# Eight experts on lists of the chosen tokens instead of on all tokens, and a first phase ordered by layer

## The reference

```python
def _ffn(x, wi, bi, wo, bo):
    return jax.nn.selu(x @ wi + bi) @ wo + bo
xf = x.reshape(-1, Hh)                                  # 2048 tokens of 128
gate_logits = _ffn(xf, gate_wi, gate_bi, gate_wo, gate_bo)   # 128 logits a token
topv, topi = jax.lax.top_k(gate_logits, K)              # K = 2 of 128
topv = topv / jnp.sum(topv, axis=-1, keepdims=True)
onehot = (topi[..., None] == jnp.arange(E)).astype(x.dtype)  # E = 8 experts
w = jnp.einsum('nk,nke->ne', topv, onehot)
h = jax.nn.selu(jnp.einsum('nh,ehf->enf', xf, exp_wi) + exp_bi[:, None, :])
out_e = jnp.einsum('enf,efh->enh', h, exp_wo) + exp_bo[:, None, :]
out = jnp.einsum('enh,ne->nh', out_e, w)
```

## Time and profile before

| | |
|---|---|
| median of 3 runs | 2991.18 us (2987.4 to 2996.92) |
| span of the profiled execution | 2973.9 us |
| PE busy | 2455.8 us (83%) |
| DVE busy | 2084.7 us (70%) |
| ACT busy | 1434.7 us (48%) |
| POOL busy | 560.2 us (19%) |
| DMA | 49.96 MB, mean 17 GB/s |

### The profile page before, as it was taken

How to read it: one execution, slowest core, us unless ns; L and a number is a source line. 1 busy time by engine, 2 the same in 40 slices (tenths; PEclk the granted TensorE clock), 3 DMA queues, 4 the chain that set the end, 5 groups by cost and what they waited for, 6 DMA issues and landing times. The chain is left out here.

```text
span 2973.9 us, 42131 instructions
## 1 busy us (share of the span) xinstructions
PE 2455.8 (83%) x16214; PEld 1563.1 (53%) x16214; DVE 2084.7 (70%) x4048; ACT 1434.7 (48%) x2603; POOL 560.2 (19%) x482
## 2 busy tenths in 40 slices
PE   5789897886797677897978869967778989789889
PEld 1257574454586322675744546835555554555554
DVE  6988887998998999998879976575572142652331
ACT  5533335884652365333358866445234434335342
POOL 2710001224792037000012205600010100000100
PEclk8999998998887679999979989978889999899999
DMA  3000000110000000000021110002000000000000
GB/s 156 0 1 1 1 1 24 42 43 12 1 1 1 0 1 0 1 28 8 1 85 42 43 62 11 2 0 52 29 1 1 1 2 1 8 1 1 1 2 7
DMA packets 28888, 49.96 MB, mean 17 GB/s; under 512 B 5264, under 2 KB 18320, under 8 KB 28176
## 3 DMA queue, kind: packets, MB, share of 16 engines
q1 hardware_dynamic: 26384, 45.17, 5.0%
q10 hardware_dynamic: 2304, 2.10, 0.3%
HBM read 26.94 MB, written 1.44 MB: 10 GB/s over the span
## 5 line engine op out<-in xcount | busy, mean ns | idle before, releaser
L146 PEld LDWEIGHTS ps<-held_ffn,hidden 128*128 128x128 f32 x2304 | 301.0, 192 | 142.4 <-issue 122.7
L164 ACT ACTIVATE grown<-ps,bias_grown 128x512 f32<-128x512 f32 x288 | 197.9, 687 | 310.5 <-PE ps L146 310.5
L146 PE MATMUL ps<-held_ffn,hidden 128*128 128x128 f32 x2304 | 305.2, 276 | 9.8 <-DVE hidden L183 9.8
L177 POOL TENSOR_TENSOR qk<-conv,held_const 128x512 f32<-128x512 f32 x64 | 89.7, 1402 | 944.4 <-DVE conv L183 944.4
L183 DVE SCALAR_TENSOR_TENSOR conv<-conv_in,held_l1a,conv 128x512 f32<-128x512 f32 x288 | 235.6, 838 | 18.7 <-ACT conv L164 15.9
L177 POOL TENSOR_TENSOR long<-long,product 128x512 f32<-128x512 f32 x136 | 198.3, 1511 | 124.5 <-ACT product L164 122.8
L183 DVE SCALAR_TENSOR_TENSOR hidden<-ps,bias_kept,grown 128x512 f32<-128x512 f32 x288 | 215.0, 748 | 7.3
L180 DVE TENSOR_SCALAR grown<-grown,bias_fallen 128x512 f32<-128x512 f32 x288 | 138.5, 481 | 59.5 <-ACT grown L164 53.2
L177 POOL TENSOR_TENSOR part<-state,c_rows 128x512 f32<-128x512 f32 x128 | 162.8, 1297 | 81.5 <-issue 34.7
L207 POOL MEMSET wide_q<- 128x1536 f32 x8 | 11.0, 1378 | 833.2 <-DVE stream_b L180 783.4
L146 PE MATMUL ps<-part,held_const 128*128 128x512 f32 x256 | 147.3, 674 | 6.9 <-POOL part L177 4.6
(11 more groups left out here) (456 smaller groups left out, 5477.5 us busy)
## 6 DMA issues: line engine op xcount, KB each, us to landing
turned<-conv SPq DMA_DIRECT2D x256, 64.0 KB, 2.0
ring<-lags SPq DMA_DIRECT2D x64, 128.0 KB
held_ffn<-in_ffn SPq DMA_DIRECT2D x1, 4690.0 KB, 17.9
held_l1a<-in_l1a SPq DMA_DIRECT2D x2, 2120.0 KB, 15.5
held_l3f<-in_l3f SPq DMA_DIRECT2D x1, 2824.0 KB, 12.2
yT<-y ACTq DMA_DIRECT2D x16, 128.0 KB, 4.9
out<-x SPq DMA_DIRECT2D x4, 256.0 KB, 2.6
held_rows<-in_rows SPq DMA_DIRECT2D x1, 788.5 KB, 7.2
```

What stands on the lines that cost most here:

```text
L146: ins = self.real.matmul(out, lhsT, rhs, **kw)
L164: return self.sent(self.real.activation(out, a, func, **kw), 0.13 + columns(out) / 1150, 0.14)
L177: return self.vector(self.real.tensor_tensor(out, a, b, op), columns(out), out, a, b)
```

## The change

1. `experts` takes both pairs of a stream at once (1024 tokens). The gate runs as before: 8 units a call.
2. A routing step follows. VectorE takes the two best logits and their places (`max`, `max_index`), builds one-hot marks, and counts with two small matmuls and two scans how many choices fall on each expert. Every choice gets a slot number; the slots of one expert fill whole tiles of 128, 23 tiles being enough in the worst case. A choice that fell on no expert gets a slot behind the 23 tiles.
3. POOL writes the normalized tokens to their slots in the chip's memory with 16 indirect DMAs of 128 rows of 512 bytes (`scatter`). SP reads the 23 tiles back (`xg`).
4. Each of the 23 tiles is one unit of another shape: 4 matmuls 128x128 up with 4 small bf16 matmuls for the bias, one exponential, one `fall` and one `selu` of 128x512, 4 matmuls 128x128 down with one bf16 matmul. Before it SP reads the tile's expert from SBUF into a register (`value`) and loads that expert's weights, 512 KB, into a ring of three places. All 23 tiles run, whether they hold tokens or not.
5. The results go to the chip's memory, and POOL fetches each choice's row with 16 indirect DMAs (`gather`). VectorE adds them to x with their weights, 16 instructions.
6. The first phase runs layer by layer: both pairs of a stream, then the next layer. The windowed attention's weights are loaded once, the filter's matrices `l2p` after both streams' second pair has left that layer. `project_channels` has two pairs in each stream in place of three and one.

The core of the diff:

```diff
+SLOT_TILES = 23
+W_RING = 3
+CHUNK = 4
+X_GROUP = [0, 0, 1, 1, 1, 1]
+SLICES = [(q, min(CHUNK, SLOT_TILES - q)) for q in range(0, SLOT_TILES, CHUNK)]
...
+        def up(j):
+            W = R.ring[:, j % W_RING, :]
+            yield pe.wait_ge(s.kept_x, j // CHUNK + 1)
+            yield pe.wait_ge(R.w_loaded[j % W_RING], w_at(j))
...
+            for c in range(FC):
+                out = tile(st.ps(j % 2), c)
+                pe.matmul(out, tile(W, c), tile(b.xgT[:, j // CHUNK % 2, :], j % CHUNK), start=True, stop=False)
+                mm = pe.matmul(out, tile(m.bias16[0:SPLIT, :], c), pick(j), start=False, stop=True)
+            mm.then_inc(s.up)
+
+        def down(j):
...
+            yield pe.wait_ge(s.hidden, GATE + j + 1)
+            if j:
+                yield pe.wait_ge(s.y_kept, j)
+            for c in range(FC):
+                pe.matmul(st.ps(2)[:, 0:P], tile(hidden, c), tile(W, FC + c), start=(c == 0), stop=False)
+            pe.matmul(st.ps(2)[:, 0:P], pick(j), tile(m.bias16[0:SPLIT, :], FC), start=False, stop=True
+                      ).then_inc(s.y_made)
...
+    def pool(po):
+        yield po.wait_ge(m.rows_clear, 64)
+        yield po.wait_ge(s.slots, 1)
+        for c in range(CHOICES):
+            h, t = divmod(c % TT, NT)
+            po.scatter(R.x, b.slots[:, c:c + 1], toks[h][:, t, :]).then_inc(R.scattered, 16)
+        for q in range(2):
+            yield po.wait_ge(R.y_stored[q], y_at(len(SLICES) - 2 + q))
+        for c in range(CHOICES):
+            po.gather(back[:, c, :], R.y, b.slots[:, c:c + 1]).then_inc(R.returned, 16)
+
+    def sync(sp):
+        def load(j):
+            row = sp.value(b.rows[0:1, j:j + 1], (E - 1) * P)
+            sp.dma_start(R.ring[:, j % W_RING, :], m.a["experts"][bass.ds(row, P), :]).then_inc(R.w_loaded[j % W_RING], 16)
+        yield sp.wait_ge(m.bias_ready, 6)
+        yield sp.wait_ge(s.rows, 1)
+        for j in range(W_RING):
+            load(j)
+        yield sp.wait_ge(R.scattered, 16 * CHOICES * (done + 1))
+        for q, (at, n) in enumerate(SLICES):
+            sp.dma_start(xg[:, at:at + n, :], R.x[at * P:(at + n) * P, :].rearrange("(t p) d -> p t d", p=P)
+                         ).then_inc(R.x_loaded[X_GROUP[q]], 16)
+        for j in range(SLOT_TILES):
+            if j + W_RING < SLOT_TILES:
+                yield sp.wait_ge(s.y_made, j + 1)
+                load(j + W_RING)
...
-    m.pairs_of = {"a": 3, "b": 1}
+    m.pairs_of = {"a": 2, "b": 2}
...
-        layers[st.name] = [layer(m, st, x(k)) for k in pairs for layer in PHASE_ONE]
+        for layer in PHASE_ONE:
+            if layer is experts:
+                layers[st.name].append(experts(m, st, [x(k) for k in pairs]))
+            else:
+                layers[st.name] += [layer(m, st, x(k)) for k in pairs]
...
     def filter_loads(sp):
-        for st in streams:
-            yield sp.wait_ge(st.x_done, 5)
+        for free in m.ring_free:
+            yield sp.wait_ge(*free)
         sp.dma_start(held["l2p"][:, :], m.a["l2p"]).then_inc(m.load["l2p"], 16)
```

More of the change, by code:

```diff
@@ L693, in tensor @@
-        yield from up(1)
-        for k in range(UNITS):
-            yield from down(k)
-            if k + 2 < UNITS:
-                yield from up(k + 2)
-        yield pe.wait_ge(s.weight, NT)
-        for t in range(NT):
-            mm = pe.transpose(st.ps(0)[0:E, tile_of(t)], b.weight[:, t, :], m.ident)
-        mm.then_inc(s.turned_w)
-        yield pe.wait_ge(s.turned_copied, 1)
-        for t in range(NT):
-            mm = pe.matmul(st.tiles(1)[:, t, :], tile(b.turned, t), w.exp_bo[0:E, :], start=True, stop=True)
@@ new lines, in tensor @@
+        yield from up_gate(1)
+        for u in range(GATE):
+            yield from down_gate(u)
+            if u + 2 < GATE:
+                yield from up_gate(u + 2)
+        yield pe.wait_ge(*m.loaded["route"])
+        yield pe.wait_ge(s.hidden, GATE)
+        yield pe.wait_ge(s.onehot, 1)
+        marks = b.onehot[:, :, :].rearrange("p e c -> p (e c)")
+        pe.matmul(totals, w.every_row, marks, start=True, stop=True).then_inc(s.counted)
+        pe.matmul(within, w.rows_before, marks, start=True, stop=True).then_inc(s.counted)
@@ L719, in vector @@
     def vector(ve):
-        yield from n_.vector(ve)
-        yield ve.wait_ge(m.load["rows"], 16)
+        for own, n_ in norms:
+            yield from n_.vector(ve)
+        yield ve.wait_ge(*m.loaded["rows"])
+        yield ve.wait_ge(*m.loaded["route"])
         yield ve.wait_ge(m.selu_ready, 3)
-        def fall(k):
-            yield ve.wait_ge(s.grown, k + 1)
-            g = b.grown[:, k % RING, :]
-            ve.tensor_scalar(g, g, SELU_ALPHA, m.bias_fallen[:, k:k + 1], ALU.min, ALU.add).then_inc(s.fell)
@@ L759, in combine @@
-        def combine(e):
-            yield ve.wait_ge(s.down, FC * (e + 1))
-            if e >= 2:
-                yield ve.wait_ge(s.combined, NT * (e - 1))
-            for t in range(NT):
-                ve.scalar_tensor_tensor(x[:, t, :], st.tiles(2 + e % 2)[:, t, :], b.scaled[:, t, e - 1:e],
-                                        x[:, t, :], ALU.mult, ALU.add).then_inc(s.combined)
-        yield from fall(0)
-        for k in range(UNITS):
-            yield from selu(k)
-            if k + 1 < UNITS:
-                yield from fall(k + 1)
-            e, f = divmod(k, FC)
-            if f == 1 and e == 1:
-                yield from gate()
-            if f == 1 and e >= 2:
-                yield from combine(e - 1)
@@ new lines, in choose @@
+        def choose(h):
+            yield ve.wait_ge(s.down, FC * (h + 1))
+            own = logits[:, NT * h:NT * h + NT, :]
+            ve.scalar_tensor_tensor(own, st.tiles(2 + h), SELU_SCALE, m.rows("gate_bo", NT), ALU.mult, ALU.add
+                                    ).then_inc(s.logits)
+            yield ve.wait_ge(s.logits, h + 1)
+            for t in range(NT * h, NT * h + NT):
+                ve.max(b.top[:, t, :], logits[:, t, :]).then_inc(s.top)
+            for t in range(NT * h, NT * h + NT):
+                yield ve.wait_ge(s.top, t + 1)
+                ve.max_index(b.found[:, t, :], b.top[:, t, :], logits[:, t, :]).then_inc(s.found)
@@ new lines, in vector @@
+        yield from fall(0)
+        for u in range(GATE):
+            yield from selu(u)
+            if u + 1 < GATE:
+                yield from fall(u + 1)
+            if u == FC + 1:
+                yield from choose(0)
+        yield from choose(1)
+        yield from route()
+        yield from fall(GATE)
+        for j in range(SLOT_TILES):
+            yield from selu(GATE + j)
+            if j + 1 < SLOT_TILES:
+                yield from fall(GATE + j + 1)
+        yield ve.wait_ge(s.weight, 1)
@@ L782, in experts @@
     st.xs += 1
-    return L.run(PE=tensor, ACT=scalar, DVE=vector)
+    return L.run(PE=tensor, ACT=scalar, DVE=vector, POOL=pool, SP=sync)
 def linear_attention(m, st, x):
```

463 lines of the change are left out of this document (330 added, 133 removed).

## The result

| | before | after |
|---|---|---|
| median of 4 runs each | 2991.98 us (2987.40 to 2996.92) | 2961.43 us (2957.25 to 2970.43) |
| ratio | | 0.9889, 95% interval 0.9854 to 0.9924 |
| span of the profiled execution | 2973.9 us | 2955.9 us |
| PE busy | 2455.8 us | 2287.9 us |
| DVE busy | 2084.7 us | 1866.6 us |

The change wins 30.5 us; 114 were forecast. The sign is right, and the time lies in the given range but outside the likeliest case's own range of 2835 to 2920. PE lost 168 us of work and the kernel gained a fifth of that, so PE now waits where it did not.

The account below looks back on a forecast made before the run. PE was taken to bound the 539 us of expert stretches, which become 394. -145 + 12 + 10 + 14 - 5 = -114 against the 2974 us span gives 2860; with 17 for the median, 2877 us, range 2795 to 3005.

Parts of the forecast that it names:

- Gate and routing, 37 us: Start of a round: 28 us of gate on PE, then 9 of routing, until stream a's slots are there.
- Scatter, s = 1.3: Token moves on POOL: each of 16 indirect DMAs takes 1.3 us; each us of s is worth 105 us.
- Rivals 1 and 2: POOL's time per indirect DMA: first, over 2.4 us, slower, chance 0.17; second, 0.6 us, 2803 us in all, chance 0.12.
- Tile, 2.3 us: Expert tiles on PE: 2.3 us each, PE staying first while both streams run, 4.6 us for a pair.
- ring of three weights covers: Expert weight loads: with both streams on, 6.9 us between `y_made` and next use cover the 5 us needed.
- Rival 3: Weight ring: loads take 8.7 us instead of 5 and set the tiles' pace, 65 us more, 2942 us; chance 0.16.
- b's gather waits for POOL and ends at 214: End of the first round: stream b's result fetch queues on POOL, done at 214 us; round's mean 206.
- its scatter and gather no longer queue behind a's: Second round: stream b comes 16 us late, so its moves find POOL free; the round costs 188 us.
- +12 for joints: Both rounds: start and end losses, 6% of the 99 us of tiles of each, 12 us lost.
- +10 for the clock: Both rounds: PE idles some 25 us before the tiles and returns at a lower clock, 5 us a round lost.
- Filter, +14: Channel mixing and delta rule: the filter, all lying there now, costs 98 us instead of 84, 14 us lost.
- rival 4: Fixed order puts one stream's waits ahead of the other's ready work, filter finds no slack: some +55, 2932 us; chance 0.09.

Follow-up runs that it names:

- no stalls: The changed kernel without the arithmetic of the state space's filter, a filter of zeros stored, on chip 11: 2850.98 us, 0.9520 of the kernel before.
- The order alone: The changed kernel's order with the kernel before's dense experts, per pair, no slot lists or moves, filter placed as in the changed kernel: 3028.21 us, ratio 1.0110.
- the run with 8 tiles: The changed kernel with 8 tiles per stream and round in place of 23: 2779.58 us on chip 11, 2816.17 us on chip 4.

## Why the prediction was right in sign and wrong in size

What failed are three terms of about 23 us each: the second round, whose moves were said not to queue on POOL and did; the new order, held at nothing; and the stalls, which had no term. The forecast of the first round was too short by 10. The unit prices (a tile, an indirect DMA, a dense unit) held.

Round 1 in us, from the gate's first matmul (at 340.3 in the profile after, 340.15 in the one without the filter, which has no stalls). "Additions done" is the end of a stream's last.

| | forecast | no stalls | after |
|---|---|---|---|
| a's slots | 37 | 44 | 44 |
| a's first tile | 65 | 71 | 71 |
| b's first tile | 86 | 93 | 101 |
| a's last tile done | 171 | 184 | 192 |
| b's last tile done | 187 | 201 | 217 |
| a's additions done | 198 | 216 | 223 |
| b's additions done | 214 | 238 | 250 |
| mean of the two ends | 206 | 227 | 236 |

- **PE sets the dense stretches:** right. The order alone, with dense experts, has PE busy for 143.6 of the 146 us of its first ones:

```profile
340.00:486.00 146.00, 143.56 (x814) 103.50 (x813) 121.57 (x281) 57.69 (x87) 0.00 (x0) 0.99 0.00 1
```

- **Gate and routing, 37 us:** 44. a's last logits came at 32 and not 28, since the gate took longer than 16 units at PE's pace, and the routing behind them took 12 and not 9: its small DVE steps were priced well (0.12 to 0.41 us each), but steps of b's gate and routing lie between them.
- **Scatter, s = 1.3:** 1.27. Rivals 1 and 2 are out by this row. The Trainium skill (SBUF, State Buffer, "A bandwidth-pool intuition that's wrong") has DVE locking GpSimd out while it writes descriptors, with 3100 ns for 620. Here the median is 0.96 us and the longest of 128 is 1.44. The profile without stalls, where more of DVE's work falls beside them, shows some of it: two scatters beside a `fall` take 1.16 and 1.18 us, and one gather of each round, beside a's additions, 2.32. All that is over 0.96 comes to 5 us for the 128, far from what rival 1 needed.

```profile
417.15 0.43 DVE L182 TENSOR_SCALAR grown<-grown 128x512 f32<-128x512 f32 x1 [1.01 <-ACT grown L166]
417.25 1.16 POOL L216 DMA_INDIRECT rows_x_b<-stream_b,slots  x1 [0.30 <-issue]
```
```profile
551.24 4.48 DVE L185 SCALAR_TENSOR_TENSOR x<-back,weight,x 128x128 f32<-128x128 f32 x16 [11.30 <-DMA back<-rows_y_a,slots]
553.75 2.32 POOL L221 DMA_INDIRECT back<-rows_y_b,slots  x1 [0.30 <-issue]
```

- **Tile, 2.3 us; ring of three weights covers:** 2.34, with PE busy 98%. Rival 3 is out. SP's part was well under the 1 us taken; its register load has a median of 0.27 us:

```profile
L226 SPq TENSOR_LOAD <-rows x92: 4/270/1072, 382.6 to 826.4; - x92
```

  The Trainium skill (DMA: Bandwidth & Descriptors, "Latency and other measured facts") gives a floor of about 600 ns; the measurement decides, and its median is below.
- **The ends of the round, "b's gather waits for POOL and ends at 214":** 238 without stalls. The walk named this wait but did not add it: 187 + 2.6 + 20.8 + 3.5 are its 214, with b's gather beginning at 190, while a's holds POOL until 194. In the run without stalls the store with its landing took 5 us and a's gather 20.3 us of POOL, so a's starts at 190 and b's at 210. In the profile after, the stalls hold b back so far that its gather, at 223, waits for its own store instead.
- **The second round, "its scatter and gather no longer queue behind a's", 188 us:** this step failed in its mechanism. The two rounds and the linear attention between them run from 340.3 to the mean first step of the window attention (853.9 and 885.8 for the streams); less the 57 us held for the attention (27 and 30, the gaps between the windows of the earlier trace rows) they are 472, so the second took 236, the same as the first. b left round 1 27 us behind a, yet its slots came only 13 us behind (681.7 against 668.4), while a scatter holds POOL for 20: b's first indirect DMA stands at 688.90, right behind a's last. The forecast's own lag of 16 us was less than its own 20.8 for a scatter, so the step did not follow even from its own numbers.
- **No term for a stall beside indirect DMAs:** 23 us of the rounds in the profile after. The run without the filter reaches the window attention at 832.7 and 859.7, on the average 23.6 earlier, with the same order of instructions up to there.
- **+12 for joints, +10 for the clock:** no run takes either apart. The granted clock is 0.76 up to a's first tile and 0.61 in the 18 us behind it, where PE resumes after 28 us without work, so it does come back at a lower one, as forecast.
- **Rounds in sum:** 394 + 12 + 10 = 416 forecast, 472 measured. 56 more: 23 are stalls, 10 belong to round 1 (227 against 206 + 11) and 23 to round 2 (222 against 188 + 11).
- **Filter, +14:** 9 to 13. **Held unchanged elsewhere:** 23 us more by the order, which no step had. Its cause is open. **`project_channels`, -5:** not measured by itself.

56 in the rounds and 27 outside (36 - 9) make the 83 us between -114 and -30.5. Of rival 4, the fixed order, a part came true: one stream's moves stand ahead of the other's on POOL. The stalls have nothing to do with it, since one and the same program has them on one chip and not on another.

"I am wrong if PE keeps its pace and the time does not fall, since then the loss lies in stretches that I held unchanged": a third of it did.

## What to carry to other kernels

Work that leaves the engine that bounds it is worth only what that engine does not then wait. Here PE lost 168 us and the kernel 30: the rounds gained 67 where 123 were forecast, and the order took 36 back. In the rounds PE waits for what runs one after the other, routing and moves; two streams with the same plan reach the moves on POOL at nearly the same time, and one waits for the other. A lag between two streams hides a queue only if it is longer than what stands in the queue (13 us against 20). And a row from the old trace prices an instruction well, but a change of order has to be run by itself: it cost 36 us, with the filter's new place, where the estimate had 9.

## What the hardware showed that was not expected

- An indirect DMA of 128 rows of 512 bytes holds POOL for 0.96 us and another 0.30 pass before the next; a plain one of 256 KB holds it for 0.75.
- On four of five chips (4, 6, 8, 13) ScalarE, and more rarely DVE and SP, stood with its inputs ready while indirect DMAs ran, ScalarE for up to 16 us at a time. On the fifth (11) it never did, in two profiles. It is worth 32 to 37 us in one program. With plain DMAs in their place it did not show on either kind of chip. A kernel with indirect DMAs can thus differ from chip to chip by more than its predecessor does, and its ratio should be taken on more than one.
- With the inputs of this case only 131 of 2048 choices fall on an expert, as counted ahead of the run with 8 tiles (the gate chooses among 128 columns, and 8 of them are experts). 15 of the 23 tiles that the worst case needs serve nobody; in two streams and two rounds these are 60 tiles, and they cost 137 to 150 us.
